# Attention block: transposes and causal triangle in 64-row tiles, query halves in two PSUM banks

## What is computed

```python
q = (x @ Wq).reshape(b, n, 16, 64).transpose(0, 2, 1, 3) * 64 ** -0.5
kv = concat([null_kv, x @ Wkv], axis=1)            # 1025 rows of 64: keys and values at once
sim = einsum('bhid,bjd->bhij', q, kv)
sim = where(causal_mask, -max, sim)
out = einsum('bhij,bjd->bhid', softmax(sim), kv)
x = x + out.reshape(b, n, 1024) @ Wout
```

## Time and profile before

| | us |
|---|---|
| three runs | 1377.71, 1378.02, 1382.98 |
| median | 1378.02 |
| span of the profiled execution | 1383.6 |
| TensorE, busy in that span | 1263.4 (91%) |
| VectorE, busy | 1114.2 (81%) |
| ScalarE, busy | 907.2 (66%) |
| GpSimd, busy | 296.4 (21%) |
| DMA, bytes moved | 69.85 MB, mean 50 GB/s |

### The profile page before, as it was taken

The page is one execution under the profiler, slowest core; times in us unless marked ns, Lnnn a source line. Parts: engine busy times, 40 slices in busy tenths (PEclk is TensorE's granted clock), DMA queues, the critical chain, the costliest instruction groups (busy, mean ns, idle before and its releaser), DMA issues. The chain is left out here.

```text
span 1383.6 us, 29418 instructions
## 1 busy us (share of the span) xinstructions
PE 1263.4 (91%) x9584; PEld 524.8 (38%) x9584; DVE 1114.2 (81%) x1937; ACT 907.2 (66%) x1879; POOL 296.4 (21%) x520
## 2 busy tenths in 40 slices
PE   4599999999979999999989999999868999999996
PEld 2122222222245555554565555555642222222222
DVE  6899999999876777777734777776668999999997
ACT  3189999988845555555533555555325999998894
POOL 4300000002003333333312333333232000000100
PEclk9689999999979999999999999999977999999998
DMA  4611122452110000000000000000043212236322
GB/s 104 209 45 55 52 62 66 93 81 78 32 35 18 18 18 18 18 18 18 18 18 18 18 18 18 18 16 1 1 137 104 63 52 54 59 77 102 71 55 61
DMA packets 53797, 69.85 MB, mean 50 GB/s; under 512 B 21264, under 2 KB 31440, under 8 KB 53712
## 3 DMA queue, kind: packets, MB, share of 16 engines
q1 hardware_dynamic: 53712, 68.75, 20.2%
HBM read 37.79 MB, written 22.54 MB: 44 GB/s over the span
## 5 line engine op out<-in xcount | busy, mean ns | idle before, releaser
L920 DVE TENSOR_REDUCE neg_max<-ps 128x1 f32<-128x1024 f32 x512 | 591.6, 1217 | 26.0 <-PE ps L1194 24.0
L756 ACT ACTIVATE arena<-ps 128x512 f32<-128x512 f32 x1024 | 545.4, 597 | 86.2 <-PE ps L1209 74.0
L1209 PE MATMUL ps<-arena 50*128 50x512 bf16 x1024 | 324.2, 389 | 15.9 <-ACT arena L756 9.9
L992 DVE TENSOR_REDUCE a_neg_max<-ps 128x1 f32<-128x129 f32 (+7 forms) x256 | 193.5, 756 | 166.3 <-PE ps L1332 164.0
L1225 PE MATMUL ps<-arena 128*32 128x256 f32 (+1 forms) x3584 | 317.3, 426 | 8.5 <-ACT arena L756 3.1
L1194 PE MATMUL ps<-arena 48*128 48x512 bf16 x1024 | 299.3, 398 | 15.0 <-DVE neg_max L920 14.0
L591 POOL TENSOR_SCALAR arena<-arena,a_rsum 128x128 f32<-128x128 f32 (+7 forms) x256 | 192.1, 750 | 416.0 <-DVE a_rsum L998 415.6
L676 ACT ACTIVATE arena<-ps,a_neg_max 128x129 f32<-128x129 f32 (+7 forms) x256 | 189.7, 741 | 73.3 <-DVE a_neg_max L992 72.8
L684 ACT ACTIVATE arena<-ps 128x128 f32<-128x128 f32 (+1 forms) x192 | 87.2, 454 | 203.8 <-PE ps L1345 203.8
L1326 PE MATMUL ps<-arena 64*128 64x321 f32 (+7 forms) x512 | 194.7, 459 | 11.7 <-ACT arena L676 9.5
L1328 PE MATMUL ps<-arena 64*128 64x128 f32 (+6 forms) x512 | 198.0, 467 | 0.0
(11 more groups left out here) (117 smaller groups left out, 850.4 us busy)
## 6 DMA issues: line engine op xcount, KB each, us to landing
arena<-stack_dram SPq DMA_DIRECT2D x128, 192.0 KB, 3.3
stack_dram<-arena SPq DMA_DIRECT2D x48, 256.0 KB, 3.6
o_dram<-arena SPq DMA_DIRECT2D x32, 256.0 KB, 2.1
arena<-arena SPq DMA_DIRECT2D x32, 256.0 KB, 3.4
arena<-o_dram SPq DMA_DIRECT2D x30, 256.0 KB, 4.2
arena<-max_dram SPq DMA_DIRECT2D x256, 1.0 KB
x<-in_L_attn_x SPq DMA_DIRECT2D x2, 512.0 KB, 5.1
max_dram<-max_T SPq DMA_DIRECT2D x64, 8.0 KB, 1.6
```

Source lines behind the costliest of these rows:

```text
L756: nc.scalar.activation(probs[:, t, :], ps[:, EXP_BANK[t], :], ACT.Exp, scale=F_SCALE).then_inc(probs_ready, 1)
L920: nc.vector.tensor_reduce(neg_max[:, g, t:t + 1], ps[:, bank:bank + 2, :].rearrange("p a b -> p (a b)"), AX, ALU.max, negate=True).then_in ...
L992: nc.vector.tensor_reduce(a_neg_max[:, t:t + 1], a_region(t), AX, ALU.max, negate=True).then_inc(a_max, 1)
L1209: ins = nc.tensor.matmul(ps[:, bank, :], stack[rows, g, 1, kt * P:(kt + 1) * P], stack[rows, g, 0, h * HALF:(h + 1) * HALF], start=True, s ...
```

## The change

Three things are done, all inside the middle layer.

- **Mask.** The 128-row matmul `ident_bf` times `causal` becomes two matmuls that use only array rows 64 to 127. `mask_sel[64:128, k]` holds a 64x64 identity at query half k, and `mask_tri[64:128, k]` the triangle for that half: 64 columns for the upper half, 128 for the lower. Both matrices are made by GpSimd at the start of the program, with one `memset` and one `affine_select` each, in place of `ident_bf` and `causal`; two semaphore counts move by one.
- **Transposes.** Each 128x128 transpose becomes two of 64 rows: queries 0 to 63 out of array rows 0 to 63 into bank 5, queries 64 to 127 out of rows 64 to 127 into bank 6, 64 columns for each key tile. So a bank now holds one query half of a whole step (up to 8 key tiles, 512 columns).
- **Copies.** VectorE copies bank 5 in every step, ScalarE bank 6 in every step, 64 columns for each key tile. The table of uses is gone. The transposes of a step wait for both copies of the step before, and `a_exps` waits for both halves of the transposes 8 steps back.

```diff
+        mask_sel = sb("mask_sel", [P, 2, P], BF16)
+        mask_tri = sb("mask_tri", [P, 2, P], BF16)
...
-                ins = nc.tensor.matmul(ps[:, mid + 1, m0:n - split], ident_bf[:, :], causal[:, :], start=False, stop=True)
+                for k in (1, 0):
+                    ins = nc.tensor.matmul(ps[:, mid + 1, m0 + k * ROWS:n - split], mask_sel[AD:P, k, :], mask_tri[AD:P, k, k * ROWS:P],
+                                           start=False, stop=k == 0)
...
             def a_transposes(pg, t):
                 qh, hh, qt = STEPS[t]
                 pe.wait_ge(a_normed, NS * pg + t + 1)
-                for k, (kt, m) in enumerate(USES[t]):
-                    use = FIRST_USE[t] + k
-
-                    if use >= 2 or not isinstance(pg, int) or pg >= 1:
-                        pe.wait_ge(evac_act if use % 2 else evac_dve, N_USES // 2 * pg + use // 2)
-                    for j in range(m):
-                        ins = nc.tensor.transpose(ps[:, T_BANK[use % 2], j * P:(j + 1) * P],
-                                                  a_probs[:, t % RING, 1 + (kt + j) * P:1 + (kt + j + 1) * P], ident[:, :])
-                    ins.then_inc(tr_done[use % 2], 1)
+                if t >= 1 or not isinstance(pg, int) or pg >= 1:
+                    pe.wait_ge(evac_dve, NS * pg + t)
+                    pe.wait_ge(evac_act, NS * pg + t)
+                for kt in range(qt + 1):
+                    for r in range(2):
+                        rows = slice(r * ROWS, (r + 1) * ROWS)
+                        ins = nc.tensor.transpose(ps[:, T_BANK[r], kt * ROWS:(kt + 1) * ROWS],
+                                                  a_probs[rows, t % RING, 1 + kt * P:1 + (kt + 1) * P], ident[rows, rows])
+                        if kt == qt:
+                            ins.then_inc(tr_done[r], 1)
...
             def a_evac(pg, t):
                 qh, hh, qt = STEPS[t]
-                for k, (kt, m) in enumerate(USES[t]):
-                    use = FIRST_USE[t] + k
-                    if use % 2 == 0:
-                        dve.wait_ge(tr_done[0], N_USES // 2 * pg + use // 2 + 1)
-                        nc.vector.tensor_copy(probs_T[qh][:, hh, kt:kt + m, (qt % 4) * P:(qt % 4 + 1) * P],
-                                              ps[:, T_BANK[0], 0:m * P].rearrange("p (k q) -> p k q", q=P)).then_inc(evac_dve, 1)
+                m, q0 = qt + 1, (qt % 4) * P
+                dve.wait_ge(tr_done[0], NS * pg + t + 1)
+                nc.vector.tensor_copy(probs_T[qh][:, hh, 0:m, q0:q0 + ROWS],
+                                      ps[:, T_BANK[0], 0:m * ROWS].rearrange("p (k q) -> p k q", q=ROWS)).then_inc(evac_dve, 1)
```

More of the change, by code:

```diff
@@ L251, in build @@
         NS = len(STEPS)
-        USES = [[(k, min(4, qt + 1 - k)) for k in range(0, qt + 1, 4)] for _, _, qt in STEPS]
-        FIRST_USE = [sum(len(USES[s]) for s in range(t)) for t in range(NS)]
         V0_STEPS = (0, 1)
@@ L476, in wait @@
                 pool.sem_inc(pool_waited, 1)
-            nc.gpsimd.memset(causal[:, :], 0.0).then_inc(const_ready, 1)
-            nc.gpsimd.tensor_copy(ident_bf[:, :], ident[:, :]).then_inc(const_ready, 1)
+            nc.gpsimd.memset(mask_tri[:, :, :], 0.0).then_inc(const_ready, 1)
+            nc.gpsimd.memset(mask_sel[:, :, :], 1.0).then_inc(const_ready, 1)
             nc.gpsimd.memset(null_sel[:, :], 0.0).then_inc(const_ready, 1)
             pool.wait_ge(const_ready, 8)
-            nc.gpsimd.affine_select(out=causal[:, :], in_=causal[:, :], compare_op=ALU.is_ge, fill=MASKED, base=0,
-                                    pattern=[[-1, P]], channel_multiplier=1).then_inc(const_ready, 1)
-            pool.wait_ge(const_ready, 9)
+            nc.gpsimd.affine_select(out=mask_tri[:, :, :], in_=mask_tri[:, :, :], compare_op=ALU.is_ge, fill=MASKED, base=-ROWS,
+                                    pattern=[[ROWS, 2], [-1, P]], channel_multiplier=1).then_inc(const_ready, 1)
+            nc.gpsimd.affine_select(out=mask_sel[:, :, :], in_=mask_sel[:, :, :], compare_op=ALU.is_equal, fill=0.0, base=-ROWS,
+                                    pattern=[[ROWS, 2], [-1, P]], channel_multiplier=1).then_inc(const_ready, 1)
+            pool.wait_ge(const_ready, 10)
             def split_rest(f):
@@ L671, in a_exps @@
                 if t >= RING or not isinstance(pg, int) or pg >= 1:
-                    before, pair = (t - RING, pg) if t >= RING else (NS + t - RING, pg - 1)
-                    use = FIRST_USE[before] + len(USES[before]) - 1
-                    act.wait_ge(tr_done[use % 2], N_USES // 2 * pair + use // 2 + 1)
+                    for r in range(2):
+                        act.wait_ge(tr_done[r], NS * pg + t - RING + 1)
                 nc.scalar.activation(a_probs[:, t % RING, 0:n], a_region(t), ACT.Exp, bias=a_neg_max[:, t:t + 1], accum_out=a_sum[:, t:t + 1]).then_inc(a_exp, 1)
@@ L679, in a_evac @@
                 qh, hh, qt = STEPS[t]
-                for k, (kt, m) in enumerate(USES[t]):
-                    use = FIRST_USE[t] + k
[L682 to L685, removed]
+                m, q0 = qt + 1, (qt % 4) * P + ROWS
+                act.wait_ge(tr_done[1], NS * pg + t + 1)
+                nc.scalar.activation(probs_T[qh][:, hh, 0:m, q0:q0 + ROWS],
+                                     ps[:, T_BANK[1], 0:m * ROWS].rearrange("p (k q) -> p k q", q=ROWS), ACT.Copy).then_inc(evac_act, 1)
             def p0_evac(b, h, bank):
@@ L1353, in a_values @@
                     last = [s for s in range(NS) if STEPS[s][0] == qh][-1]
-                    done = (FIRST_USE[last] + len(USES[last])) // 2
-                    pe.wait_ge(evac_dve, N_USES // 2 * pg + done)
-                    pe.wait_ge(evac_act, N_USES // 2 * pg + done)
+                    pe.wait_ge(evac_dve, NS * pg + last + 1)
+                    pe.wait_ge(evac_act, NS * pg + last + 1)
                     pe.wait_ge(pv_bank_free, k0)
```

7 lines of the change are left out of this document (2 added, 5 removed).

## The result

The changed kernel takes 1366.58 us, the median of four runs (1365.37 to 1370.68); the kernel before takes 1377.87 (1376.62 to 1382.98). The ratio is 0.9907 with a 95% interval of 0.9883 to 0.9932: 11.3 us faster by the medians, where 24 us were forecast. The profiled execution took 1365.37 us with a span of 1363.2.

A forecast was written before the change was run, and what follows sets the result against it. TensorE was taken to set the pace; 2.4 - 0.5 + 3.5 = 5.4 us a pair gained less 3.5 to 4.0 of waits, say 1.6, over fifteen pairs 24 us: 1378 - 24 = 1354 us, range 1340 to 1368.

The forecast's parts named there:

- the size of a pair: Middle layer: a pair of heads was to take about 32.2 us after the change, against 33.85 before.
- the clock: Rival: waits of steps 15 and 0 halve TensorE's clock for 10.2 us, costing 3.4 in ten pairs: 1388 us; chance 0.17.
- Mask, 0.5 us a pair: Mask of each step: the added 64-column matmul costs 0.03 us, 16 x 0.03 = 0.5 us a pair.
- shape changes, 2.4: TensorE between scores, mask, transposes, values and queries: fewer losses where the tile shape changes, 2.4 us a pair gained.
- Transposes, 0.06 us a key tile: 72 key tiles a pair: two half transposes run together at 0.06 us, gaining 72 x 0.049 = 3.5 us.
- The rival that the halves gain nothing: Transposes: loads take 0.11 a pair or follow each other, so the 3.5 is gone; say 1380 us; chance 0.17.
- The new wait, 4.9 us a pair with 1.4 there before: Transposes wait for VectorE's copy behind a maximum: 4.9 us a pair over eight steps, so 3.5 to 4.0 come back.
- the copy of the output: VectorE's output copy (0.68, step 13) was to add up to 0.5 us a pair to the new waits.
- Sum, 1.6 us a pair: Net gain in the middle layer: 5.4 us gained, 3.5 to 4.0 returned, say 1.6 us a pair.
- Against it: with 0.17, 0.35 and 0.40 idle in each pair the clock stayed at 1.00: Sign against a falling clock: TensorE's three stalls in each pair of the kernel before left the clock at full.
- The 1.00 of a whole pair: Clock of a pair with 72 transposes, read as not bearing out that transposes do not bring up the full clock.
- Fifteen pairs: Middle layer: the gain counted for fifteen of 16 pairs, as the first lacks transposes in its first four steps: 24 us.

The follow-up runs named there:

- the two experiments: Kernel before with the 64-row mask alone: ratio 1.0029; changed kernel with the old 128-row mask, so transposes and copies alone: ratio 1.0043.
- the second profile of before: The kernel before, run once more unchanged for another profile: 1377.48 us, span 1375.5.
- one half after the other: Changed kernel with all transposes of query half 0 first, then all of half 1: 1377.88 us, ratio 0.999.

## Why the prediction was right, and where not

The direction, the mechanism and the size of a pair were right, the last in part by luck; the total was 12.6 us too low, most of it because one step, the clock, was missized. It still lies inside the 1340 to 1368 of the forecast itself, but that range was made for slower loads, not for the clock.

- **Mask, 0.5 us a pair, and shape changes, 2.4.** The mask is right: its second matmul starts 0.03 us behind the first, and the mask alone costs 0.44 a pair. The shape changes are right in kind, as the two experiments show, but 0.5 too large (see the sum).
- **Transposes, 0.06 us a key tile.** Right, and the decisive choice: 0.18 us for three tiles. The rival that the halves gain nothing would have made each pair 33.8. The rule of the Trainium skill weighed there ("TensorE: Matmul & The Clock Gate", LDWEIGHTS), 107 ns for a load of 128 columns, does not hold for these loads: two of them go by in 60 ns.
- **The new wait, 4.9 us a pair with 1.4 there before.** Right in kind, 0.8 too large in size. TensorE's waits in the pair that starts at 468.81 are

```profile
PE ps L1339 <- issue: 1.9, 5, 0.6
PE ps L1339 <- DVE arena L1001: 1.0, 2, 0.8
PE ps L1318 <- ACT arena L672: 0.4, 1, 0.4
```

  By the prediction's own measure, idle time plus 0.17 for each modelled end, the transposes wait 1.9 + 1.0 + 7 x 0.17 = 4.1 us. The table below says the same: it counts from the start of the second mask matmul, and 0.06 of that is no wait, as step 11 shows. Four of the eight steps agree within 0.05. Step 15 is 0.40 longer by the copy of the output, which the prediction named but gave no place: it holds the maximum of step 14 up to 566.40. Step 0 is 0.38 shorter, so the two together come out as forecast (1.75 against 1.73), for which the prediction gave no reason: that is luck. At step 11 TensorE comes late by itself, since its scores still wait for an exponential as in the earlier trace rows, and has no wait ahead of the transposes; why step 12 is 0.3 shorter was not followed up. That these waits were the price is shown from two sides: values in their place take 1.33 us off a pair, and moving the copy moves them.
- **Sum, 1.6 us a pair.** Right, 1.62 at full clock, but two errors cancel in it. The waits ahead of transposes grew to 4.1 from the 0.35 + 0.17 + 2 x 0.17 = 0.86 of the earlier trace rows, so 3.3 us were returned where 3.5 to 4.0 were forecast. TensorE's work shrank by that and by the 1.62: 4.9 us, where 5.4 were forecast. With 72 x 0.049 = 3.5 for the transposes and 0.5 lost on the mask, 1.9 of the 4.9 are left for the shape changes, not 2.4; that the scores' load still shows is part of the difference.
- **The clock: the step that failed.** The prediction had it as a rival, a case apart, at 0.17: in the main either no pair falls or most do (ten in its price, 0.06 of the 0.17 with fewer), at 3.4 us each from the 10.2 us stretch of the earlier trace rows. It is neither. The stalls of steps 15 and 0 do bring half clock, in four of 13 ordinary pairs, but for 3.4 us, and each costs 1.62. "Against it: with 0.17, 0.35 and 0.40 idle in each pair the clock stayed at 1.00" was the wrong comparison, since the change about doubles two of these stalls (with the 0.17 of a modelled end, 0.34 to 0.81 and 0.52 to 0.94). The price was wrong too: I took off the waits inside a stretch, 1.7 of 5.1 us. There are hardly any, as the waits are over when the stretch begins. Two measurements say so: 3.4 us cost 1.62, 10.2 us cost 4.7, each nearly half of the length. The 1.00 of a whole pair, which the prediction also read as a sign about transposes, says little of them: 72 at 0.109 us are 7.8 of its 33.85 us.
- **Fifteen pairs.** Between the second profile of before and that of after, the stretch from the first score of pair 1 to that of pair 16 fell from 533.5 to 518.4 us, by 15.1: 13 pairs at 1.62 less four low stretches at 1.62 are 14.6, the first and the output-projection pair give 0.8 (35.58 to 35.33 and 57.33 to 56.78). The latter I had counted at 1.6; it has a low stretch too, at 711.0. The last pair has one at 929.5: from its first score to its last transpose it takes 39.84 us in place of 40.36, so 0.5 of its 1.6 is left. Six low stretches at 1.62 are 9.7 us, and that is about what the middle layer lacks of the 24.
- **Layers behind.** The spans differ by 1375.5 - 1363.2 = 12.3, not 15.1. The first score came 0.8 us earlier (401.25 against 402.05; the 425 named further up as the layer's start is too late), and the work from the last pair's first score on took 443.6 us in place of 439.9. In ten profiles that stretch lies between 439.9 and 445.5. What follows the last transpose is not changed; here it is for the first and the second profile of the kernel before and for the changed kernel:

```profile
980.40:1383.57 403.17, 362.23 (x3127) 118.55 (x3125) 356.54 (x430) 301.05 (x565) 48.07 (x124) 0.94 0.29 72
975.92:1375.50 399.58, 359.48 (x3127) 118.08 (x3125) 356.41 (x430) 301.01 (x565) 47.89 (x124) 0.95 0.29 73
959.44:1363.18 403.74, 363.39 (x3132) 118.06 (x3127) 356.66 (x430) 301.05 (x565) 49.01 (x124) 0.94 0.29 72
```

  In the trace the clock is at half for 51.2, 41.0 and 51.4 us of these. The kernel before has the long and the short form, so the 4 us need no effect of the change; why an execution has one or the other stays open.

The new wait by step, from the start of the second mask matmul to the first transposes, in the pair that starts at 468.81:

| step | 3 | 8 | 10 | 11 | 12 | 14 | 15 | 0 | sum |
|---|---|---|---|---|---|---|---|---|---|
| forecast, us | 0.42 | 0.43 | 0.47 | 0.40 | 0.96 | 0.50 | 0.42 | 1.31 | 4.91 |
| measured, us | 0.43 | 0.45 | 0.49 | 0.06 | 0.70 | 0.51 | 0.88 | 0.99 | 4.51 |
| less 0.06, us | 0.37 | 0.39 | 0.43 | 0 | 0.64 | 0.45 | 0.82 | 0.93 | 4.03 |

## What to carry to other kernels

When buffers that the steps used in turn are all filled in every step, list for each step what the consumer's engine does between two fills, and look for work that can stand in the gap: here the same change is worth 11 us with the old order and 42 with the values moved ahead of the waits. Price the stalls twice, once by their length and once by what two of them close together do to TensorE's clock; a low stretch costs nearly half its length, and the same stalls bring it in some repetitions and not in others. Two edits that each lose can gain together where the cost lies in the change between shapes, so such parts are to be tried together.

## What was not expected of the hardware

- TensorE starts matmuls of different row halves out of program order: with one half after the other, scores at 568.32 ahead of transposes at 568.38 and 568.44 that stand before them; in the changed kernel, a transpose at 556.63 ahead of a mask matmul that stands before it. The Trainium skill ("TensorE: Matmul & The Clock Gate", Part 3, The mechanism) says that matmuls start and end in program order; for tiles in different row halves the starts in these rows show otherwise.
- The half clock came in stretches of 3.4 us after a turn in which TensorE was busy for 1.47 of 2.89 us, and not each time; with 3.06 of 3.70 it never came in 13 pairs.
- A pair of 64x64 float32 transposes with their loads goes by in 0.06 us, where one 128x128 takes 0.11.
